# A hybrid block's kernel on one core: the decay cut by a minimum, one PE loop and all loops of the convolution written out, a normalisation moved to ACT

## The chip, the cores and the metric

The kernel runs on one core of a Trainium2 chip. The metric is device time in microseconds (us) from one launch. A core has five engines with a queue each: TensorE (PE in the profile; PEld is its weight loads), VectorE (DVE), ScalarE (ACT), GpSimd (POOL) and SyncE (SP, which only issues transfers). Each engine works through its own list in order and waits on semaphores.

## What is computed

```python
x = x + attn_a(layernorm(x))   # x: 8 x 2048 x 256
x = x + ffn(layernorm(x))
x = x + attn_b(layernorm(x))
x = x + ffn(layernorm(x))

# attn_a, the scan, per head (8 heads, P=64, N=128):
alpha = exp(dt_t * A_neg); beta = (1 - lam_t) * dt_t * alpha; gamma = lam_t * dt_t
Bx_t = u_t[:, :, :, None] * Bp_t[:, :, None, :]
h = alpha * h + beta * Bx_prev + gamma * Bx_t
y_t = einsum('bhpn,bhn->bhp', h, Cp_t)
# attn_b: projection to 3 x 256 channels, short filter of 3 taps, gates, and per channel
y = irfft(rfft(vx, n=2L) * rfft(k, n=2L))[..., :L]       # a causal convolution over 2048 tokens
# ffn:
r = sigmoid(xr @ W_r.T); k = square(relu(xk @ W_k.T)); out = r * (k @ W_v.T)
```

## The kernel before

The work is in stages that follow each other: normalise the tokens and compute the scan's parameters and the long filter (0 to 311 us); the mixer with the first feed-forward part (`mixer_and_first_ffn`); the long convolution (`long_convolution`); projection and second feed-forward part (`project_and_second_ffn`). Between stages data go through DRAM.

**Mixer.** A tile is 128 tokens, a quad is four tiles; there are 128 tiles and 32 quads. The eight heads are worked on in two groups g of four. Per tile and group POOL multiplies `steps` (L1076) out of the logarithms of the decay; PE sums them over tokens in `decay_logs` (L752, L753) and adds a mask of -30000 above the diagonal by a bf16 matmul with `ident_b` (L754); ACT takes the exponential (`exponentials`, L933) and scales the identity by rho (`own_diagonal`, L940); POOL adds the two (`add_own`, L1090); DVE multiplies the result with the Gram matrix (`weigh_gram`, L1208). Around them PE projects B and C (L744) and u (L761), DVE rotates (`rotate`, L1194, L1195), POOL adds the rotated halves (L1085), PE turns them (L769) for the Gram matrices (L779), and so on. Per quad the feed-forward part and the projection of attn_b are mixed in: `xn_over` (L826), `key` (L833), `value`, `x2n_over` (L858), `widen` (L865); DVE's `mix_tokens` (L1250) makes the `x_rk` that `key` reads. The order on each engine is written out by hand in its `body(tile, quad, n)`: `tile(q, lag, step)` calls a step for the tile that lies `lag` behind. `rounds` runs the body for four quads written out, then in a loop whose body holds two quads (14 turns), then for the last quads and two more to empty the pipeline.

**Long convolution.** 256 channels are worked on in 128 pairs. Per pair SP loads two shifted copies of the taps into one of 8 slots `toep` (`fill`), a quarter of the rows each time; DVE and ACT copy the other rows (`copy_upper`, L1369, L1370), two pairs ahead. PE transposes the signal (`signal_over`, L1482), ACT copies it (`copy_signal`, L1419), PE does 64 matmul calls over 32 lags, in the profile 128 records of each pair (`convolve`, L1498), ACT copies the odd half (`copy_odd_sums`, L1427), DVE adds the halves (`sum_halves`, L1538), PE transposes back (`back_over`, L1511), DVE adds the skip and gates (`skip_and_gate`, L1551, L1555). Four channels share a buffer `vt`, `x0t`, `yv` (four of each): in ACT's queue `store` waits until DVE has gated them, issues the store (L1412), and then `fetch` issues two loads (L1407, L1408) for the buffers that come free. All engines but POOL loop over 8 pairs per turn: the first 8 and, on all but SP, the last 8 pairs are written out.

**Last stage.** Per tile: PE projects (L1740), POOL has added a bias to the residual (L1673), DVE adds and takes the statistics (L1788 to L1795), POOL raises to the power -1/2 (L1679), DVE normalises (L1801), PE transposes (L1748), ACT copies, POOL takes differences (L1694), DVE mixes (L1809), PE multiplies (L1757, L1760, L1768), ACT and DVE finish. POOL's order is bias, difference of two tiles before, power, first column (L1687) of the tile before.

## Time and profile before

| what | value |
|---|---|
| time, median of 3 runs | 5024.38 us (5023.03 to 5030.68) |
| profiled execution | 5031.85 us, of which the span of instructions is 5030.1 us |
| mean granted TensorE clock | 0.942 of full speed |
| PE busy | 4415.2 us (88%), 40180 matmul records, and as many weight loads |
| DVE busy | 3076.4 us (61%) |
| POOL busy | 2557.7 us (51%) |
| ACT busy | 2076.3 us (41%) |

Busy time is the time in which the engine carried out instructions; semaphores, branches and the issue of transfers do not count. A name such as SPq or ACTq is the engine's queue, where transfers are issued. Behind an instruction, "idle before <-X" says how long its engine was idle just before it and what ended that; "issue" stands where nothing that the profile shows was waited for. L and a number is the line of the kernel.

### The profile page before, as it was taken

The page shows a single profiled execution, that of the slowest core. Times are in us where ns is not written, and L with a number is a line of the kernel's source. Part 1 is how long each engine was busy: PE and PEld are TensorE (multiplying, and loading weights), DVE is VectorE, ACT ScalarE, POOL GpSimd, SP SyncE. Part 2 cuts the span into 40 slices and gives each one's busy share as a digit, 9 for nine tenths or more (in the row PEclk, how much of TensorE's full clock was granted, in tenths as well). Part 3 has the DMA queues.
Part 4 walks back from the last instruction along what each step waited for, and adds up shares of the span by engine and source line. Part 5 has one row for each costly group of instructions (what it writes and reads, how often), then busy time and mean ns, then how long its engine had stood idle before and what let it go on. Part 6 is the DMA issues. An engine that isn't in the chain of part 4 may idle for free. (4 is left out here: it accounts for less than half of the span.)

```text
span 5030.1 us, 118987 instructions
## 1 busy us (share of the span) xinstructions
PE 4415.2 (88%) x40180; PEld 3573.1 (71%) x40180; DVE 3076.4 (61%) x6634; ACT 2076.3 (41%) x4921; POOL 2557.7 (51%) x3276
## 2 busy tenths in 40 slices
PE   5259999899999999999999999999668888889999
PEld 4037777777777777777777777777556777768887
DVE  8545665566656665666566665666444545459998
ACT  3123444444434444444434443444344555543333
POOL 3047666666666666676666666766200000005555
PEclk9569999999999999999999999999888999989999
DMA  8120111111111111111111111111065555543332
GB/s 265 67 78 27 40 35 43 40 41 35 44 34 39 40 35 42 39 40 35 43 40 41 35 44 34 37 40 32 28 163 138 147 148 145 142 109 97 99 100 91
DMA packets 369520, 348.52 MB, mean 69 GB/s; under 512 B 24665, under 2 KB 342937, under 8 KB 359833
## 3 DMA queue, kind: packets, MB, share of 16 engines
q1 hardware_dynamic: 250652, 273.54, 18.2%
q10 hardware_dynamic: 118272, 67.12, 5.0%
q8 instruction: 363, 5.95, 0.5%
q14 instruction: 233, 1.91, 0.1%
HBM read 231.91 MB, written 108.66 MB: 68 GB/s over the span
## 5 line engine op out<-in xcount | busy, mean ns | idle before, releaser
L744 PE MATMUL bank<-w_bc,xnT 128*128 128x512 f32 x3072 | 823.8, 410 | 85.1 <-POOL xnT L1068 40.3
L744 PEld LDWEIGHTS bank<-w_bc,xnT 128*128 128x128 f32 x3072 | 559.6, 189 | 223.0 <-issue 77.2
L949 ACT COPY turned_t<-bank 128x512 f32<-128x512 f32 x512 | 299.5, 585 | 959.8 <-PE bank L769 959.7
L1194 DVE TENSOR_TENSOR rot<-bank,par 128x512 f32<-128x512 f32 x512 | 353.2, 690 | 460.2 <-POOL turned_c L1085 245.4
L1498 PE MATMUL p_yc<-sig,toep 64*64 64x256 f32 (+14 forms) x16384 | 577.6, 293 | 57.0 <-issue 42.9
L1498 PEld LDWEIGHTS p_yc<-sig,toep 64*64 64x64 f32 x16384 | 502.0, 138 | 149.8 <-issue 106.5
L1076 POOL TENSOR_TENSOR steps<-upto,par 128x512 fp32r<-128x512 f32 x512 | 521.9, 1041 | 0.0
L1663 POOL MEMSET xT<- 128x258 f32 x1 | 0.3, 313 | 855.3 <-POOLq L1376 855.3
L1068 POOL TENSOR_TENSOR xnT<-xnT_raw,xnT 128x256 fp32r<-128x256 f32 x128 | 101.5, 793 | 542.9 <-ACT xnT L928 542.9
L1195 DVE TENSOR_TENSOR rot<-bank,par 128x512 f32<-128x512 f32 x512 | 348.5, 681 | 0.0
L1085 POOL TENSOR_TENSOR turned_b<-rot 128x512 f32<-128x512 f32 x256 | 326.1, 1274 | 41.9 <-DVE rot L1195 41.5
L1538 DVE TENSOR_TENSOR ys<-p_yc,odd_y 64x256 f32<-64x256 f32 x256 | 95.6, 411 | 402.6 <-ACT odd_y L1427 399.2
L1090 POOL TENSOR_TENSOR decay<-decay,own 128x512 f32<-128x512 f32 x256 | 329.0, 1285 | 11.3 <-ACT decay L933 10.7
L1085 POOL TENSOR_TENSOR turned_c<-rot 128x512 f32<-128x512 f32 x256 | 327.5, 1279 | 2.3 <-DVE rot L1195 2.3
L940 ACT ACTIVATE own<-ident,par 128x128 f32<-128x128 f32 x1024 | 327.4, 403 | 0.1
L865 PE MATMUL bank<-x2T,in_w 128*128 128x512 f32 x1152 | 309.7, 405 | 12.4 <-issue 5.9
L779 PEld LDWEIGHTS bank<-turned_t 128*128 128x128 f32 x2048 | 297.4, 209 | 15.8 <-issue 0.4
L1277 DVE SCALAR_TENSOR_TENSOR conv<-bank,short,conv 128x511 f32<-128x511 f32 (+1 forms) x384 | 285.9, 745 | 33.9 <-ACT conv L1005 18.8
L779 PE MATMUL bank<-turned_t 128*128 128x128 f32 x2048 | 295.9, 292 | 0.2 <-DVE u_g L1202 0.2
L1122 POOL TENSOR_TENSOR rstd<-var_eps,minus_half 128x2 f32<-128x2 f32 x128 | 90.4, 706 | 404.1 <-DVE var_eps L1234 404.1
L1208 DVE TENSOR_TENSOR mix<-bank,decay 128x512 f32<-128x512 f32 x256 | 175.5, 686 | 156.3 <-PE bank L779 156.3
L805 PEld LDWEIGHTS bank<-u_w,turned_b 128*128 128x128 f32 x2048 | 248.5, 192 | 22.1 <-issue 14.8
(258 smaller groups left out, 9780.6 us busy)
## 6 DMA issues: line engine op xcount, KB each, us to landing
toep<-taps_dram SPq DMA_DIRECT2D x256, 260.0 KB, 4.2
el<-el_dram SPq DMA_DIRECT2D x256, 128.0 KB, 3.1
xg<-arg_x SPq DMA_DIRECT2D x32, 512.0 KB, 4.7
xnT_dram<-xt_g ACTq DMA_DIRECT2D x32, 512.0 KB, 3.9
xnT_raw<-xnT_dram SPq DMA_DIRECT2D x128, 128.0 KB, 2.9
x_quad<-arg_x SPq DMA_DIRECT2D x32, 512.0 KB, 4.3
x_dram<-x_quad SPq DMA_DIRECT2D x32, 512.0 KB, 3.2
x0T_dram<-conv SPq DMA_DIRECT2D x32, 512.0 KB, 2.8
```

Of the source, the lines that this page charges most:

```text
L744: last = mm(p_bc[c][:, :], xnT[w.q % 2][p][:, k, :], w_bc[q][:, k, c * 1024 + g * W4:c * 1024 + (g + 1) * W4], start=(n == 0), stop=(n == ...
L779: last = mm(p_gram[:, c], turned_t[g][0][:, c], turned_t[g][1][:, c], start=True, stop=True)
L865: last = mm(p_post[W_BANK[e]][:, :], in_w[q][:, k, e * 128:(e + 1) * 128], x2T[p][:, k, :], start=(m == 0), stop=(m == len(SPLIT) - 1))
L940: last = s_.activation(own[g][:, h * TOK:(h + 1) * TOK], ident[:, :], ACT.Identity, scale=par[w.p][:, w.q, P_RHO + g * GROUP + h:P_RHO + g ...
L949: s_.copy(turned_t[g][c][:, :], p_tr[:, :]).then_inc(s[f"copy_{BC[c]}"], 1)
L1076: last = g_.tensor_tensor(heads(steps[p][:, :]), upto[:, :].unsqueeze(1).broadcast_to([128, GROUP, TOK]), over(of_group(P_A + p * HEADS, w ...
L1085: g_.tensor_tensor(turned(w, g, c)[:, :], rot1[c][:, :], rot2[c][:, :], ALU.add).then_inc(s[f"turn_{BC[c]}"], 1)
L1090: g_.tensor_tensor(decay[g][:, :], decay[g][:, :], own[g][:, :], ALU.add).then_inc(s["own"], 1)
L1194: v_.tensor_tensor(heads(rot1[c][:, :]), heads(p_bc[c][:, :]), cos, ALU.mult)
L1195: v_.tensor_tensor(parts(rot2[c][:, :]), parts(p_bc[c][:, :])[:, :, ::-1, :], over(sin.rearrange("p (h s) -> p h s", s=2), STATE // 2), AL ...
L1277: last = v_.scalar_tensor_tensor(out=conv[:, e, back:], in0=p_post[W_BANK[e]][:, 0:SPAN - back], scalar=short[:, e, 2 - back:3 - back], in ...
L1498: last = mm(by_seq(p_y[p][c][odd * H:(odd + 1) * H, 0:2 * TILES])[:, :, first:], toep[place % SLOTS][c * H:(c + 1) * H, lag * H:(lag + 1) ...
```

## The change

It consists of four edits.

1. The mask is no longer in the logarithms. POOL builds a constant `bound` (1 on the diagonal, 0 on one side of it, 1e38 on the other), ACT scales it by rho, held above zero by a floor of 1e-30, in place of the identity (`own_bounds`), and the exponential and this bound are joined by a minimum on DVE (`cut_decay`) in place of POOL's addition. `cut_decay` for group 1 of the tile before stands after DVE's first rotation; that for group 0 before `gate_values`. PE's mask matmul goes.
2. PE's list in the mixer is written out for all quads.
3. The convolution has no loops on any engine. SP issues the loads of `vt` and `x0t` and the stores too, between its fills.
4. In the last stage `normalise` moves from DVE to ACT, at the end of ACT's list for a tile; POOL computes `shift` = -mean * rstd for it behind the power.

```diff
-            g_.affine_select(out=t["mask"][:, :], in_=t["mask"][:, :], compare_op=ALU.is_ge, fill=0.0,
-                             base=0, pattern=[[-1, 128]], channel_multiplier=1)
             pool.drain()
-            g_.tensor_copy(t["ident_b"][:, :], t["ident"][:, :])
+            g_.tensor_tensor(t["bound"][:, :], t["upto"][:, :], t["ident"][:, :], ALU.subtract)
+            pool.drain()
+            g_.tensor_scalar(t["bound"][:, :], t["bound"][:, :], BEYOND, None, ALU.mult)
+            pool.drain()
+            g_.tensor_tensor(t["bound"][:, :], t["bound"][:, :], t["ident"][:, :], ALU.add)
...
-            v_.tensor_tensor(col(P_RHO), as3(arr["gam"][:, :]), as3(arr["e1"][:, :]), ALU.mult)
+            v_.scalar_tensor_tensor(out=col(P_RHO), in0=as3(arr["gam"][:, :]), scalar=TINY, in1=as3(arr["e1"][:, :]), op0=ALU.max, op1=ALU.mult)
...
+        if unrolled:
+            for n in range(QUADS + 2):
+                one(n, n % 2)
+            return
...
                 mm(p_arg[:, :], after_r[:, :], steps[0][:, :], start=True, stop=False)
-                mm(p_arg[:, :], after_r[:, :], steps[1][:, :], start=False, stop=False)
-                mm(p_arg[:, :], ident_b[:, :], mask[:, :].unsqueeze(1).broadcast_to([128, GROUP, TOK]),
-                   start=False, stop=True).then_inc(s["logs"], 1)
+                mm(p_arg[:, :], after_r[:, :], steps[1][:, :], start=False, stop=True).then_inc(s["logs"], 1)
...
-            rounds(pe, body)
+            rounds(pe, body, unrolled=True)
...
                 for h in range(GROUP):
-                    last = s_.activation(own[g][:, h * TOK:(h + 1) * TOK], ident[:, :], ACT.Identity,
+                    last = s_.activation(own[g][:, h * TOK:(h + 1) * TOK], bound[:, :], ACT.Identity,
                                          scale=par[w.p][:, w.q, P_RHO + g * GROUP + h:P_RHO + g * GROUP + h + 1])
...
-            def add_own(i, w, g):
-                wait_for(pool, f"diagonal{g}", i)
-                wait_for(pool, f"exp{g}", i)
-                g_.tensor_tensor(decay[g][:, :], decay[g][:, :], own[g][:, :], ALU.add).then_inc(s["own"], 1)
...
-                    tile(q, 1, add_own, 1)
...
-                    tile(q, 0, add_own, 0)
...
+            def cut_decay(i, w, g):
+
+                wait_for(dve, f"diagonal{g}", i)
+                wait_for(dve, f"exp{g}", i)
+                v_.tensor_tensor(decay[g][:, :], decay[g][:, :], own[g][:, :], ALU.min).then_inc(s["own"], 1)
...
                     tile(q, 0, rotate, 0, 1)
+                    tile(q, 1, cut_decay, 1)
                     tile(q, 0, rotate, 0, 0)
...
                     tile(q, 1, take_y, 1)
+                    tile(q, 0, cut_decay, 0)
                     tile(q, 0, gate_values)
...
+            flat = {n: t[n].rearrange("c t n -> (c t n)") for n in ("vxT_dram", "x0T_dram", "yT_dram")}
+            QUAD = U * TILES * TOK
+            rows = lambda name, m: flat[name][m * QUAD:(m + 1) * QUAD].rearrange("(u t n) -> t u n", u=U, t=TILES)
+
+            def fill(n):
+                slot = n % SLOTS
+                wait(sp, conv_ready, n - SLOTS + 1)
+                for c in range(2):
+                    src = taps[(2 * n + c) * ROW + H:(2 * n + c + 1) * ROW]
+                    sp.dma_start(toep[slot][c * H:c * H + QTR, :], bass.AP(src.tensor, src.offset, [[1, QTR], [1, SEQ + QTR]])).then_inc(toep_in[slot], 16)
+
+            def fetch(m):
+                wait(sp, yv_ready, U * (m - Q + 1))
+                sp.dma_start(vt[m % Q][:, :, :], rows("vxT_dram", m)).then_inc(quad_in[m % Q], 16)
+                sp.dma_start(x0t[m % Q][:, :, :], rows("x0T_dram", m)).then_inc(quad_in[m % Q], 16)
+
+            def store(m):
+                wait(sp, yv_ready, U * (m + 1))
+                sp.dma_start(rows("yT_dram", m), yv[m % Q][:, :, :]).then_inc(yv_out[m % Q], 16)
+
             sp.dma_start(skip[:, :], t["filt_bias"].partition_broadcast(128)).then_inc(skip_in, 16)
-
-            def fill(it, place):
-                n = BODY * it + place
-                slot, free = place % SLOTS, at(n - SLOTS + 1)
-                offs = [at((2 * n + c) * ROW + H) for c in range(2)]
-                wait(sp, conv_ready, free)
-                for c in range(2):
-                    src = taps[bass.ds(offs[c], ROW - H)]
-                    rows = bass.AP(src.tensor, src.offset, [[1, QTR], [1, SEQ + QTR]])
-                    sp.dma_start(toep[slot][c * H:c * H + QTR, :], rows).then_inc(toep_in[slot], 16)
-            for place in range(BODY):
-                fill(0, place)
-            with sp.Fori(1, ITERS) as it:
-                for place in range(BODY):
-                    fill(it, place)
+            fill(0)
+            fetch(0)
+            for n in range(1, SLOTS):
+                fill(n)
+                if n < Q:
+                    fetch(n)
+            for n in range(SLOTS, PAIRS + 2 * (Q + 1)):
+                if n < PAIRS:
+                    fill(n)
+                m = n // 2 - (Q + 1)
+                if n % 2 == 0 and m >= 0:
+                    store(m)
+                    if m + Q < QUADS:
+                        fetch(m + Q)
+            for p in range(Q):
+                sp.wait_ge(yv_out[p], 16 * QUADS // Q)
...
-            def body(it, first=False, last=False):
-                for place in range(BODY):
-                    n = BODY * it + place
-                    copy_signal(n, place % 2)
-                    if not (last and place + AHEAD >= BODY):
-                        copy_upper(act, "act", nc.scalar.copy, it, place + AHEAD)
-                    if not (first and place == 0):
-                        copy_odd_sums(n - 1, (place - 1) % 2)
-                    q = place // 2
-                    if place % 2 == 1 and not (first and q == 0):
-
-                        off, off_next, done = at((Q * it + q - 1) * QUAD), at((Q * it + q + Q - 1) * QUAD), at((Q * it + q) * U)
-                        slot = (q - 1) % Q
-                        store(off, slot, done)
-                        if not (last and q > 0):
-                            fetch(off_next, slot, done)
-            for q in range(Q):
-                fetch(q * QUAD, q, 0)
-            for place in range(AHEAD):
-                copy_upper(act, "act", nc.scalar.copy, 0, place)
-            body(0, first=True)
-            with act.Fori(1, ITERS - 1) as it:
-                body(it)
-            body(ITERS - 1, last=True)
-            copy_odd_sums(PAIRS - 1, 1)
-            store((Q * ITERS - 1) * QUAD, Q - 1, DIM)
-            for p in range(Q):
-                act.wait_ge(yv_out[p], 16 * ITERS)
+            for n in range(AHEAD):
+                copy_upper(act, "act", nc.scalar.copy, n)
+            for n in range(PAIRS):
+                copy_signal(n, n % 2)
+                if n + AHEAD < PAIRS:
+                    copy_upper(act, "act", nc.scalar.copy, n + AHEAD)
+                if n > 0:
+                    copy_odd_sums(n - 1, (n - 1) % 2)
+            copy_odd_sums(PAIRS - 1, (PAIRS - 1) % 2)
...
-            signal_over(0, 0)
-            body(0, first=True)
-            with pe.Fori(1, ITERS - 1) as it:
-                body(it)
-            body(ITERS - 1, first="last")
-            back_over(ITERS - 1, BODY - 1)
+            signal_over(0)
+            for n in range(PAIRS):
+                if n + 1 < PAIRS:
+                    signal_over(n + 1)
+                convolve(n)
+                if n > 0:
+                    back_over(n - 1)
+            back_over(PAIRS - 1)
...
-                g_.tensor_tensor(rstd[p][:, :], var_eps[p][:, :], t["minus_half"][:, 0:1], ALU.pow).then_inc(s["rstd2nd"], 1)
+                g_.tensor_tensor(rstd[p][:, :], var_eps[p][:, :], t["minus_half"][:, 0:1], ALU.pow)
+                g_.tensor_tensor(minus_mean[:, :], mean_var[p][:, 0:1], minus_one[:, :], ALU.mult)
+                pool.drain()
+                g_.tensor_tensor(shift[p][:, :], minus_mean[:, :], rstd[p][:, :], ALU.mult).then_inc(s["rstd2nd"], 1)
...
+            def normalise(g, v):
+                i, p = R * g + v, v % 2
+                wait_for(act, "rstd2nd", i)
+                wait_for(act, "xn2nd_over", i - 2)
+                s_.activation(xn[p][:, :], x3[v % R][:, :], ACT.Identity, scale=rstd[p][:, :], bias=shift[p][:, :]).then_inc(s["norm2nd"], 1)
...
+                on(0, normalise)
...
-            def normalise(g, v):
-                i, p = R * g + v, v % 2
-                wait_for(dve, "rstd2nd", i)
-                wait_for(dve, "xn2nd_over", i - 2)
-                v_.tensor_scalar(xn[p][:, :], x3[v % R][:, :], mean_var[p][:, 0:1], rstd[p][:, :], ALU.subtract, ALU.mult).then_inc(s["norm2nd"], 1)
...
-                on(0, normalise)
```

The matmul, transpose and copy steps of the convolution keep their contents; only their indices are constants now.

## Rows read from the trace of the kernel before

**Rows 1.** Busy time by stage: start:end, length, each engine's busy us (instructions), clock, DMA share, GB/s.

```profile
311.00:3652.00 3341.00, 3079.54 (x19072) 2488.24 (x19072) 1992.57 (x3651) 1403.19 (x3268) 2230.97 (x2708) 0.97 0.12 38
3652.00:4507.60 855.60, 698.91 (x17408) 592.00 (x17408) 417.91 (x1024) 432.54 (x1024) 0.27 (x2) 0.91 0.55 142
4507.60:5030.10 522.50, 508.17 (x2816) 422.36 (x2816) 464.17 (x1408) 175.95 (x512) 287.48 (x516) 0.98 0.32 97
```

The engines of these rows are PE, PEld, DVE, ACT and POOL, in this order.

**Rows 2.** Timeline of the convolution, PE's transposes: start us, length, instruction, idle before.

```profile
3690.33 0.63 PE L1482 MATMUL p_sig<-ident,vt 128*64 128x128 f32 x4
3695.32 0.63 PE L1482 MATMUL p_sig<-ident,vt 128*64 128x128 f32 x4
...
3777.81 0.70 PE L1482 MATMUL p_sig<-ident,vt 128*64 128x128 f32 x4 [3.60 <-issue]
...
4492.09 0.62 PE L1482 MATMUL p_sig<-ident,vt 128*64 128x128 f32 x4
```

**Rows 3.** Timeline, ACT's signal copy ahead of the third of these.

```profile
3775.08 0.87 ACT L1419 COPY sig<-p_sig 64x128 f32<-64x128 f32 x4 [5.57 <-issue]
```

**Rows 4.** Timeline, a stop of PE within one pair's matmuls.

```profile
3756.17 0.53 PE L1498 MATMUL p_yc<-sig,toep 64*64 64x48 f32 x22 [0.63 <-issue]
```

**Rows 5.** Timeline, PE's first convolution.

```profile
3683.36 1.13 PE L1498 MATMUL p_yc<-sig,toep 64*64 64x256 f32 x8 [12.29 <-ACT sig L1419]
```

**Rows 6.** Timeline of the mixer, PE from the logarithms to the Gram matrix.

```profile
2013.70 0.39 PE L752 MATMUL bank<-steps,after_r 128*128 128x512 f32 x1
...
2017.18 1.05 PE L779 MATMUL bank<-turned_t 128*128 128x128 f32 x8
```

**Rows 7.** Waits of PE in the mixer: us in total, times, longest.

```profile
PE bank L752 <- POOL steps L1076: 43.5, 30, 1.6
...
PE bank L833 <- DVE x_rk L1250: 29.9, 32, 3.1
```

**Rows 8.** Timeline of the last stage, one matmul group per tile.

```profile
4832.01 1.03 PE L1760 MATMUL bank<-w_r_sb,x_r 128*128 128x256 f32 x4
...
4859.94 1.03 PE L1760 MATMUL bank<-w_r_sb,x_r 128*128 128x256 f32 x4
...
4863.64 1.03 PE L1760 MATMUL bank<-w_r_sb,x_r 128*128 128x256 f32 x4
```

**Rows 9.** Timeline of the mixer, POOL's addition.

```profile
2021.82 1.26 POOL L1090 TENSOR_TENSOR decay<-decay,own 128x512 f32<-128x512 f32 x1
```

**Rows 10.** Groups by shape: busy us in all, mean ns of one, idle before.

```profile
L1801 DVE TENSOR_SCALAR xn<-x,mean_var,rstd 128x256 f32<-128x256 f32 x128 | 91.9, 718 | 1.3 <-POOL rstd L1679 1.3
...
L1290 DVE TENSOR_TENSOR vx<-conv 128x1024 f32<-128x1024 f32 x32 | 39.2, 1227 | 4.4 <-issue 3.9
```

**Rows 11.** Timeline of the mixer, first transposes of three quads in a row.

```profile
1049.50 0.63 PE L826 MATMUL bank<-ident,xn 128*128 128x128 f32 x4
...
1152.45 0.63 PE L826 MATMUL bank<-ident,xn 128*128 128x128 f32 x4
...
1254.30 0.63 PE L826 MATMUL bank<-ident,xn 128*128 128x128 f32 x4
```

**Rows 12.** Timeline: POOL in the mixer, then DVE and POOL in the last stage.

```profile
2026.32 0.70 POOL L1122 TENSOR_TENSOR rstd<-var_eps,minus_half 128x2 f32<-128x2 f32 x1
...
2027.33 0.20 POOL L1125 TENSOR_TENSOR shift<-minus_mean,rstd 128x2 f32<-128x2 f32 x1
...
4527.60 0.42 DVE L1788 TENSOR_TENSOR x<-bank,x 128x256 f32<-128x256 f32 x1 [0.43 <-PE bank L1740]
...
4529.09 0.63 POOL L1679 TENSOR_TENSOR rstd<-var_eps,minus_half 128x1 f32<-128x1 f32 x1 [0.48 <-DVE var_eps L1795]
...
4529.85 0.84 POOL L1673 TENSOR_TENSOR x<-x,out_b 128x256 f32<-128x256 f32 x1
```

**Rows 13.** Busy time in ten microseconds of the convolution, columns as in rows 1.

```profile
3700.00:3710.00 10.00, 10.00 (x273) 8.83 (x273) 4.88 (x14) 5.69 (x15) 0.00 (x0) 1.00 0.69 189
```

**Rows 14.** DMA queues: packets, MB, share of 16 engines.

```profile
q8 instruction: 363, 5.95, 0.5%
```

More of the change, by code:

```diff
@@ L491, in mixer_and_first_ffn @@
     SPAN = QUAD * TOK
-    ident, ident_b, upto, after, mask = t["ident"], t["ident_b"], t["upto"], t["after"], t["mask"]
+    ident, upto, after, bound = t["ident"], t["upto"], t["after"], t["bound"]
     w_u, w_bc = [sb(f"w_u{p}", [128, KT, 512], F32R) for p in range(2)], [sb(f"w_bc{p}", [128, KT, 2048], F32R) for p in range(2)]
@@ L640, in mixer_and_first_ffn, with rounds @@
     Place = namedtuple("Place", "n q p")
[L642 removed]
+    def rounds(eng, body, unrolled=False):
         def one(n, u):
@@ L1013, in body @@
                     tile(q, 2, square_y)
-                    tile(q, 0, own_diagonal, 0)
+                    tile(q, 0, own_bounds, 0)
                     if q == 3:
@@ L1029, in body @@
                     tile(q, 0, exponentials, 0)
-                    tile(q, 0, own_diagonal, 1)
+                    tile(q, 0, own_bounds, 1)
                     if q == 0:
@@ L1410, in store @@
-            def store(off, q, done):
-                wait(act, yv_ready, done)
-                act.dma_start(rows("yT_dram", off), yv[q][:, :, :]).then_inc(yv_out[q], 16)
             def copy_signal(n, p):
@@ L1512, in back_over @@
                 last.then_inc(back_ready, 1)
-            def body(it, first=False):
-                for place in range(BODY):
-                    nxt = (it, place + 1) if place + 1 < BODY else (it + 1, 0)
-                    prev = (it, place - 1) if place else (it - 1, BODY - 1)
-                    if not (first == "last" and place == BODY - 1):
-                        signal_over(*nxt)
-                    convolve(it, place)
-                    if not (first is True and place == 0):
-                        back_over(*prev)
-            signal_over(0, 0)
-            body(0, first=True)
-            with pe.Fori(1, ITERS - 1) as it:
-                body(it)
-            body(ITERS - 1, first="last")
-            back_over(ITERS - 1, BODY - 1)
+            signal_over(0)
[6 more added lines that the diff above has]
+            back_over(PAIRS - 1)
         @block.vector
@@ L1555, in skip_and_gate @@
                     v_.tensor_tensor(yv[q][:, 2 * p + c, :], skipped[2 * p + c][:, :], x0t[q][:, 2 * p + c, :], ALU.mult).then_inc(yv_ready, 1)
-            at_n = lambda n: n if isinstance(n, int) else dve.snap(n)
             dve.wait_ge(skip_in, 16)
-            def body(it, first=False, last=False):
-                for place in range(BODY):
-                    n = BODY * it + place
-                    if not (last and place + AHEAD >= BODY):
-                        copy_upper(dve, "dve", nc.vector.tensor_copy, it, place + AHEAD)
-                    sum_halves(n, place % 2)
-                    if not (first and place == 0):
-                        skip_and_gate(*((it, place - 1) if place else (it - 1, BODY - 1)))
-            for place in range(AHEAD):
-                copy_upper(dve, "dve", nc.vector.tensor_copy, 0, place)
-            body(0, first=True)
-            with dve.Fori(1, ITERS - 1) as it:
-                body(it)
-            body(ITERS - 1, last=True)
-            skip_and_gate(ITERS - 1, BODY - 1)
+            for n in range(AHEAD):
+                copy_upper(dve, "dve", nc.vector.tensor_copy, n)
+            for n in range(PAIRS):
+                if n + AHEAD < PAIRS:
+                    copy_upper(dve, "dve", nc.vector.tensor_copy, n + AHEAD)
+                sum_halves(n, n % 2)
+                if n > 0:
+                    skip_and_gate(n - 1)
+            skip_and_gate(PAIRS - 1)
 def project_and_second_ffn(nc, ctx, t):
@@ L1833, in build @@
         const = lambda name, dt=F32: ctx.enter_context(nc.sbuf_tensor(name, [128, 128], dt))
-        for n in ("ident", "upto", "after", "ones", "nxt", "wrap"):
+        for n in ("ident", "upto", "after", "ones", "nxt", "wrap", "bound"):
             t[n] = const(n)
-        t["mask"], t["ident_b"] = const("mask", BF16), const("ident_b", BF16)
         t["minus_half"] = ctx.enter_context(nc.sbuf_tensor("minus_half", [128, 4], F32))
```

65 lines of the change are left out of this document (25 added, 40 removed).

## The prediction

> **What bounds the kernel now.** I read the busy time by stage first [rows 1]. Three stages matter: the mixer (311 to 3652 us), the long convolution (3652 to 4508) and the last stage (4508 to 5030). In each PE is the busiest engine, but not equally: 3079.54 of 3341 us in the mixer (92%), 698.91 of 855.6 in the convolution (82%), 508.17 of 522.5 in the last. So the convolution has the most idle PE time, though two of the four edits are elsewhere.
>
> *Convolution.* I took the timeline of PE and followed one instruction that comes once per pair of channels, the transpose of line 1482 [rows 2]. Near the start, in code written out before the loop, two pairs are 3695.32 - 3690.33 = 4.99 us apart; no pair is shorter while PE works through, so 4.99 is PE's floor. From 3690.33 to 4492.09 there are 126 steps, 6.36 us on average. PE therefore loses 1.37 us per pair, 126 x 1.37 = 173 us. The long stops look like the third of rows 2: 3.60 us of idle PE. What came late is ACT's copy of the signal, which ended at 3775.95 after 5.57 us in which ACT computed nothing [rows 3]. In that time ACT's queue stood in `store` (it waits for DVE's products) and then issued three transfers. ACT is thus late because it issues, not because it is full: 432.54 us busy of 855.6 [rows 1]. A smaller kind of stop lies inside one pair's matmuls, where no semaphore is: 0.63 us before the last 22 of 128 [rows 4]. I read it as late code. The stage also starts slowly: PE's first convolution waits 12.29 us for ACT's signal copy, behind eight loads that ACT issues first [rows 5].
>
> *Mixer.* The fp32r matmuls follow each other steadily. From 2013.70 to 2017.18 there are 15 (two of the logarithms, the mask, twelve of the projection): 3.48 / 15 = 0.232 us each, the mask's among them [rows 6]. In the list of waits PE stands 43.5 us for POOL's `steps` (30 times) and 29.9 us for DVE's `x_rk` (32 times) [rows 7].
>
> *Last stage.* The matmul of line 1760 comes once per tile: 31.63 us for eight tiles, 3.954 each, but 3.70 in the one case where DVE was on time [rows 8]. DVE is busy 464.17 of 522.5 us and PE mostly waits for it.
>
> **The change part by part, in us.**
>
> 1. *Convolution: transfers to SP, no loops.* ACT no longer stands in `store` or issues; its work per pair is 432.54 / 128 = 3.4 us [rows 1], inside the 4.99. Its copies then come early in each pair. If nothing else appears, the 173 go. SP takes over: a `store` is queued behind a `fill` and waits for the gate of a pair one before the one that the fill waited for, so it holds SP briefly. Behind it stand the next fills, which have some five pairs (25 us) until they are needed; the fetches have four (20 us). Loop branches go on all engines. What I keep is the late code inside pairs. A stop of 0.63 in two pairs of five is 0.25 per pair, 127 x 0.25 = +32. Bounds: 0, and 0.63 in each pair, +80. The start gives back the 12.29 us [rows 5], -12 (0 if SP's queue fills up as ACT's did). Sum: -173 + 32 - 12 = **-153**, bounds -185 and -93.
>
>    The Trainium skill, "Runtime: NRT & Kernel Launch", section "Instruction fetch mechanics", says that fetch is sequential, that crossing a block is mostly hidden, and that a taken branch forces a fetch. By it the +32 would be nothing. The row of 0.63 in code without a branch [rows 4] does not agree with "mostly hidden", so I do not follow it.
>
> 2. *Mixer: mask matmul and POOL's add out, DVE's minimum in.* PE loses 256 matmuls (two per tile) of 0.232 us: -59. It counts almost fully, as PE is busy 92% and no other engine above 67% [rows 1]; bounds -59 and -30. POOL loses 256 adds of 1.26 us [rows 9]. At each start of a quad one of them stands ahead of the sums and of `steps`, for which PE waits 43.5 us in total [rows 7]: 30 x 1.26 = -38, bounds 0 and -43. DVE gains 256 minima of 128x512. The nearest row between two SBUF tiles is 1227 ns for 128x1024 [rows 10], 0.61 each: 157 us, DVE goes from 60% to 65%. Most lie in DVE's idle time, but before the `x_rk` for which PE waits [rows 7] one adds its full length: 32 x 0.61 = +20. `cut_decay` also waits for ACT's exponential, and behind it on DVE stand a rotation and the residual of an earlier quad. At the start of a quad ACT is late, so this delays the mix; I give it +10. Bounds for DVE together: 0, and half of the 157, +80. ACT's `own_bounds` costs what `own_diagonal` did.
>
> 3. *Mixer: PE without its loop.* The first transpose of line 826 marks a quad of tiles: 102.95 us, then 101.85 [rows 11]. They alternate so, and the loop's body holds two quads, so I read 1.10 us as the branch: 14 turns, -15; bounds 0 and -15.
>
>    Mixer: -59 - 38 + 20 + 10 - 15 = **-82**, bounds -117 and +50.
>
> 4. *Last stage: `normalise` from DVE to ACT.* DVE loses 0.718 us per tile [rows 10]: from 464.17 / 128 = 3.63 of work to 2.91. ACT is busy 175.95 of 522.5 us and holds the new operation easily. PE's floor is 3.70 [rows 8]. POOL gets a product, a drain and a second product. The same sequence in the mixer takes 2027.33 + 0.20 - 2026.32 = 1.21 us, where the power alone takes 0.70: +0.51 [rows 12]. This closes a ring: DVE's sum and statistics (4527.60 to 4529.09), POOL's power, first column and bias (4529.09 to 4530.69), then DVE's next sum. It is 3.09 now, some 0.1 more for the hand-over, so 3.19 + 0.51 = 3.70 after: level with PE. I take 3.73: 124 x (3.954 - 3.73) = **-28**, bounds -31 and -10.
>
> 5. *The constants* (POOL builds `bound` in place of the mask) and the floor under rho: three small operations more, before the first transposes need anything of them, and one operation of the same size. Nothing.
>
> Sum: -153 - 82 - 28 = -263. The profiled execution spans 5030.1 us and took 5031.85; the median of the runs is 5024.38, 7.5 lower. The span should be near 4767 and the time **4761 us**.
>
> **The rivals.**
>
> *A. As worked out*, 4761, with its own range 4700 to 4820. For it: the pairs of 4.99 exist in this trace.
>
> *B. The transfers limit the convolution.* At 5.25 us per pair the DMA engines would be busy 0.55 x 6.36 / 5.25 = 0.67 of the time, and code has to pass among them. Against it: from 3700 to 3710 they were busy 0.69 at 189 GB/s and PE worked 10.00 of 10 us [rows 13]. If two thirds of the gain stay out: 4761 + 102 = 4863.
>
> *C. The minimum takes back the mixer's gain.* DVE works in order, and a minimum that waits for ACT holds up rotations that PE needs. For it: the late ACT at each start of a quad. Against it: DVE is idle 40%. Mixer 0: 4761 + 82 = 4843.
>
> *D. The shorter stop keeps TensorE's clock up.* The granted clock is 0.97 in the mixer [rows 1]; after the stop at the start of a quad it is at the lower of its two levels for some microseconds. If it stayed at the upper one, 3% of 3341 = 100 us would come back: 4761 - 100 = 4661.
>
> *E. Slower: code written out arrives too late.* PE's mixer and convolution, and all engines of the convolution, now run through their code once. One mechanism with one price: a stop of 0.63 us [rows 4] at each piece of code. The instruction queue moved 363 packets for the larger of the two streams [rows 14]; if each cost PE another 0.73 us, the gain of 263 would be gone, and at 1 us the time is 4761 + 363 = 5124. Against it: that stream holds 5.95 MB, 74 bytes for each of PE's 2 x 40180 records, so the loops' code seems to have been moved anew on each turn already.
>
> **How the numbers follow.** A 0.60, B 0.11, C 0.13, D 0.12, E 0.04. The range 4660 to 4850 holds A, C and the upper edge of D, and leaves out most of B and D and all of E. 0.2% is about what a measurement of this kernel can tell from no change (10 us). Faster: A to D and a little of E, 0.96. Within 0.2%: 0.01. Slower: 0.03.
>
> **What the profile of the changed kernel would show.** Step 1: the transposes of the signal about 5.2 us apart, ACT without transfers, the stage some 700 us long. A spacing above 6 with stops inside the matmuls speaks for B or E, stops in front of them for a late queue of SP. Step 2: no matmul with the mask, PE's wait for `steps` far below 43.5, the quads about 100 us apart; 102 or more means C, with PE waiting for DVE's `rot` or `x_rk`; a granted clock of 0.99 or 1.00 means D. Step 3: even spacing of the quads. Step 4: 3.7 us per tile; 3.8 or more, with PE waiting behind POOL's `shift`, means that the ring closes later than I think. The prediction is wrong above all if stops inside PE's matmuls grow, or if DVE is late in the mixer.

## The result: 4827.57 us, and where the 198 us came from

The changed kernel takes 4827.57 us (median of 4 runs, 4820.36 to 4829.95), the kernel before 5025.49 in the same comparison (4 runs, 5023.03 to 5030.68): a ratio of 0.9602, with a 95% interval from 0.9586 to 0.9619. It is 198 us faster. The forecast was 4761, so 263 faster, with a range of 4660 to 4850.

The busy time by stage of the changed kernel (stretch, length, then PE, PEld, DVE, ACT and POOL busy, granted clock, DMA share, GB/s), to be read against [rows 1]:

```profile
311.00:3642.39 3331.39, 3061.74 (x18816) 2507.80 (x18816) 2150.42 (x3907) 1397.99 (x3268) 1981.20 (x2448) 0.96 0.12 38
3642.39:4329.00 686.61, 653.88 (x17408) 564.24 (x17408) 417.11 (x1024) 433.09 (x1024) 0.57 (x2) 0.98 0.66 176
4329.00:4828.20 499.20, 484.97 (x2816) 426.17 (x2816) 424.38 (x1280) 252.04 (x640) 321.58 (x773) 0.98 0.33 102
```

| stage | before | after | measured | forecast |
|---|---|---|---|---|
| mixer | 3341.0 | 3331.4 | -9.6 | -82 |
| convolution | 855.6 | 686.6 | -169.0 | -153 |
| last stage | 522.5 | 499.2 | -23.3 | -28 |

The convolution and the last stage did what was forecast. The mixer did not: PE has 256 matmuls fewer in it (18816 against 19072), POOL 260 instructions fewer, and it is hardly shorter.

*Convolution.* PE's timeline in the changed kernel, to be read against [rows 2, 5]:

```profile
3652.30 1.89 PE L1468 MATMUL p_sig<-ident,vt 128*64 128x128 f32 x8 [18.71 <-DMA x0t<-x0T_dram]
3657.07 3.36 PE L1483 MATMUL p_yc<-sig,toep 64*64 64x256 f32 x32 [2.89 <-ACT sig L1426]
...
3674.41 2.43 PE L1483 MATMUL p_yc<-sig,toep 64*64 64x184 f32 x92 [2.22 <-issue]
...
3677.17 0.62 PE L1468 MATMUL p_sig<-ident,vt 128*64 128x128 f32 x4
...
4309.54 0.63 PE L1468 MATMUL p_sig<-ident,vt 128*64 128x128 f32 x4
...
4314.54 0.63 PE L1468 MATMUL p_sig<-ident,vt 128*64 128x128 f32 x4
```

Two pairs are 4314.54 - 4309.54 = 5.00 apart when nothing stops PE, and from 3677.17 to 4314.54 there are 123 steps of 5.18 on average. The first matmul of a convolution starts 14.7 us into the stage (3657.07 - 3642.39), before 31.7 (3683.36 - 3651.68). PE's 17408 instructions of the stage take 653.88 us in place of 698.91 [rows 1], at a granted clock of 0.98 in place of 0.91: 45 of the 169 us are the same work done faster, the rest is idle time that went.

*Mixer.* PE's waits in the mixer (total, times, longest), to be read against [rows 7]:

```profile
PE bank L747 <- DVE rot L1189: 52.4, 30, 3.8
PE bank L770 <- issue: 49.8, 25, 5.1
...
PE bank L755 <- POOL steps L1077: 34.0, 31, 1.3
PE bank L834 <- DVE x_rk L1250: 27.8, 32, 3.0
PE bank L866 <- issue: 15.6, 31, 3.0
PE bank L780 <- issue: 13.5, 29, 1.3
```

The wait for `steps` fell from 43.5 to 34.0 only; the wait for `rot` is the longest of the mixer's repeated ones; and there are more waits that end on nothing shown ("issue"): 13.5 us in front of line 780, where the kernel before (its line 779) had 0.2 us of idle time in all. Not every such wait is a new one: the kernel before lost 66.8 us in front of its line 769 (the 770 here), of which the profile puts 52.5 down to ACT's `turned_t`, and run 1 below, with PE's loop, has 11.6 us in front of line 780, of which 9.9 are put down to DVE's `mix`. The quads (the four tiles between two such rows) still alternate, against [rows 11]:

```profile
1965.19 0.63 PE L827 MATMUL bank<-ident,xn 128*128 128x128 f32 x4 [0.50 <-DVE conv L1277]
...
2066.93 0.63 PE L827 MATMUL bank<-ident,xn 128*128 128x128 f32 x4 [0.50 <-issue]
2067.90 0.63 PE L827 MATMUL bank<-ident,xn 128*128 128x128 f32 x4 [0.34 <-issue]
...
2170.02 0.63 PE L827 MATMUL bank<-ident,xn 128*128 128x128 f32 x4 [0.50 <-DVE conv L1277]
```

101.74 and 103.09 us, though PE has no loop any more.

*Last stage.* PE's line 1740, once per tile, against [rows 8]:

```profile
4429.97 1.03 PE L1740 MATMUL bank<-w_r_sb,x_r 128*128 128x256 f32 x4
...
4433.70 1.03 PE L1740 MATMUL bank<-w_r_sb,x_r 128*128 128x256 f32 x4
...
4437.40 1.03 PE L1740 MATMUL bank<-w_r_sb,x_r 128*128 128x256 f32 x4
...
4441.21 1.03 PE L1740 MATMUL bank<-w_r_sb,x_r 128*128 128x256 f32 x4
...
4456.03 1.03 PE L1740 MATMUL bank<-w_r_sb,x_r 128*128 128x256 f32 x4
...
4460.00 1.03 PE L1740 MATMUL bank<-w_r_sb,x_r 128*128 128x256 f32 x4
```

Eight tiles take 30.03 us, 3.75 each: most steps are 3.70, one is 3.81 and one 3.97, once per loop turn of eight tiles. PE's weight loads waited 39.2 us in total for DVE's `x_k` before (93 times, line 1757); now they wait 12.9 (45 times, line 1737).

### The profile page after: what moved, and what is told of

The parts are those of the page before. It is cut to its first block and busy times, and to the rows that moved or that the text cites. A ratio compares the mean times of both kernels' runs of the same rounds, so it can differ in the third digit from the quotient of the medians.

```text
span 4828.2 us, 121179 instructions
## 1 busy us (share of the span) xinstructions
PE 4325.3 (90%) x39924; PEld 3566.1 (74%) x39924; DVE 3193.5 (66%) x6762; ACT 2149.7 (45%) x5049; POOL 2345.0 (49%) x3277
## 5 line engine op out<-in xcount | busy, mean ns | idle before, releaser
L1483 PE MATMUL p_yc<-sig,toep 64*64 64x256 f32 (+14 forms) x16384 | 539.6, 282 | 14.5 <-issue 10.3
L1483 PEld LDWEIGHTS p_yc<-sig,toep 64*64 64x64 f32 x16384 | 476.2, 132 | 90.9 <-issue 44.2
L1077 POOL TENSOR_TENSOR steps<-upto,par 128x512 fp32r<-128x512 f32 x512 | 537.3, 1069 | 0.0
L941 ACT ACTIVATE own<-bound,par 128x128 f32<-128x128 f32 x1024 | 326.9, 402 | 0.2 <-DMA par<-params_dram 0.2
L780 PEld LDWEIGHTS bank<-turned_t 128*128 128x128 f32 x2048 | 287.4, 206 | 52.1 <-issue 31.9
L780 PE MATMUL bank<-turned_t 128*128 128x128 f32 x2048 | 298.0, 293 | 14.3 <-issue 13.5
L866 PEld LDWEIGHTS bank<-x2T,in_w 128*128 128x128 f32 x1152 | 215.9, 192 | 74.0 <-issue 24.2
L966 ACT ACTIVATE xn<-x_quad,shift,rstd 128x256 f32<-128x256 f32 x256 | 136.7, 593 | 266.8 <-POOL shift L1121 266.8
```

Source lines behind the costliest of these rows:

```text
L780: last = mm(p_gram[:, c], turned_t[g][0][:, c], turned_t[g][1][:, c], start=True, stop=True)
L866: last = mm(p_post[W_BANK[e]][:, :], in_w[q][:, k, e * 128:(e + 1) * 128], x2T[p][:, k, :], start=(m == 0), stop=(m == len(SPLIT) - 1))
L941: last = s_.activation(own[g][:, h * TOK:(h + 1) * TOK], bound[:, :], ACT.Identity, scale=par[w.p][:, w.q, P_RHO + g * GROUP + h:P_RHO + g ...
L1077: last = g_.tensor_tensor(heads(steps[p][:, :]), upto[:, :].unsqueeze(1).broadcast_to([128, GROUP, TOK]), over(of_group(P_A + p * HEADS, w ...
L1483: last = mm(by_seq(p_y[p][c][odd * H:(odd + 1) * H, 0:2 * TILES])[:, :, first:], toep[n % SLOTS][c * H:(c + 1) * H, lag * H:(lag + 1) * H] ...
```

## The experiments

A stage ends here with SyncE's first transfer in the next; the mixer is counted from 311 us on, as above. This agrees with the table above within 1 us. All in us; the kernel before took 5024.9 to 5028.5 in the comparisons; "ratio" is to the kernel before, with its 95% interval.

| kernel | time | ratio | mixer | conv. | last |
|---|---|---|---|---|---|
| before | 5025 | 1 | 3340.7 | 855.9 | 522.5 |
| changed | 4827.6 | 0.9602 [0.9586, 0.9619] | 3331.4 | 687.6 | 498.2 |
| min_only | 4966.3 | 0.9876 [0.9860, 0.9893] | 3288.0 | 852.1 | 522.2 |
| pe_unrolled_only | 5028.9 | 1.0011 [1.0001, 1.0020] | 3378.7 | 810.7 | 522.8 |
| conv_act_issues | 4937.9 | 0.9824 [0.9808, 0.9841] | 3340.8 | 758.0 | 526.4 |
| conv_sp_issues | 4962.5 | 0.9868 [0.9852, 0.9885] | 3340.7 | 788.6 | 522.0 |
| after_pe_looped | 4779.4 | 0.9507 [0.9492, 0.9523] | 3285.5 | 682.4 | 498.0 |
| after_mixer_unrolled | 4799.3 | 0.9541 [0.9525, 0.9557] | 3300.1 | 688.9 | 499.0 |
| min_mask_kept | 5023.7 | 0.9990 [0.9981, 1.0000] | 3335.1 | 852.5 | 522.2 |
| no_mask_only | 4962.8 | 0.9874 [0.9857, 0.9890] | 3284.0 | 833.1 | 522.0 |
| no_add_only | 5390.5 | 1.0729 [1.0707, 1.0750] | 3694.6 | 856.8 | 529.5 |
| no_add_free | 4996.4 | 0.9947 [0.9930, 0.9963] | 3295.5 | 854.9 | 529.2 |
| conv_code_moved | 5056.8 | 1.0064 [1.0043, 1.0085] | 3340.1 | 883.9 | 522.1 |
| last_stage_unrolled | 4776.7 | 0.9512 [0.9491, 0.9532] | 3285.1 | 684.9 | 491.9 |

**1. min_only.** Of the change only the mixer's arithmetic: mask out, minimum on DVE; all loops stay.

```diff
-                mm(p_arg[:, :], after_r[:, :], steps[1][:, :], start=False, stop=False)
-                mm(p_arg[:, :], ident_b[:, :], mask[:, :]..., start=False, stop=True).then_inc(s["logs"], 1)
+                mm(p_arg[:, :], after_r[:, :], steps[1][:, :], start=False, stop=True).then_inc(s["logs"], 1)
...
-                    tile(q, 1, add_own, 1)      # POOL
...
+                    tile(q, 1, cut_decay, 1)    # DVE
...
```

> The kernel before with one part alone: the mask matmul and POOL's add are gone from the mixer and DVE takes the minimum; all loops stay, the convolution and the last stage are as before. Theory T (in each second quad of tiles DVE's and ACT's loop branches of about 3 and 2 us stand on PE's path, and what PE saves elsewhere is waited off there, partly as a longer stretch at the lower clock): the mixer is 8 to 12 us shorter than before, all of it in the quads written out. Rival P (the terms of my prediction): 67 us shorter. Rival C (the minimum on DVE takes the gain back): 0 or longer, with PE waiting more for rot and x_rk in every quad, written out or not.

The mixer became 52.7 us shorter. Theory T falls, rival C too; the prediction's term (67) was nearly right in size. So what the changed kernel lacks is lost by the other part.

**2. pe_unrolled_only.** Of the change only PE's mixer without its loop.

```diff
-            rounds(pe, body)
+            rounds(pe, body, unrolled=True)
```

> The kernel before with one part alone: PE's mixer without its loop; mask matmul, POOL's add, the convolution and the last stage as before. Theory T: the mixer is 0 to 2 us shorter and the quads still alternate by 1.1 us, because it is DVE's and ACT's branch that makes them alternate. Rival P: 15 us shorter and the quads evenly spaced.

Neither: the mixer is 38.0 us longer. Quads in the stretch where the other engines loop are 103.0 and 105.2 us apart, before 101.8 and 102.9. PE's 19072 instructions take 3107.54 us in place of 3079.54 [rows 1]: 28 of the 38 are the same work done slower, 10 are idle. The granted clock of the turn quad shows it. First this kernel, then the kernel before (stretch, length, PE busy, granted clock, DMA share, GB/s):

```profile
2138.00:2143.00 5.00, 1.61 (x10) 1.00 0.04 11
2143.00:2154.00 11.00, 8.24 (x42) 0.53 0.20 61
2154.00:2160.00 6.00, 6.00 (x42) 1.00 0.00 0
```

```profile
2123.00:2129.00 6.00, 2.68 (x12) 1.00 0.01 3
2129.00:2133.00 4.00, 3.07 (x11) 0.57 0.53 164
2133.00:2140.00 7.00, 7.00 (x58) 1.00 0.00 0
```

After its stops at the start of the quad PE works for 11 us almost wholly at the lower of its two levels (1.2 GHz), where the looped PE had 4. Over the whole mixer the clock is 0.95 against 0.97 [rows 1]. The stop in front is longer, 3.39 us for DVE's `rot` against 2.47, and DVE itself stands there for its own loop's turn ("issue"), as it did before. Again this kernel first:

```profile
2140.41 0.69 DVE L1198 TENSOR_TENSOR rot<-bank,par 128x512 f32<-128x512 f32 x1 [3.19 <-issue]
...
2141.85 1.67 PE L748 MATMUL bank<-w_bc,xnT 128*128 128x512 f32 x6 [3.39 <-DVE rot L1199]
```

```profile
2122.32 0.69 DVE L1194 TENSOR_TENSOR rot<-bank,par 128x512 f32<-128x512 f32 x1 [3.04 <-issue]
...
2123.66 1.67 PE L744 MATMUL bank<-w_bc,xnT 128*128 128x512 f32 x6 [2.47 <-DVE rot L1195]
```

The convolution, whose code is the same, is 45 us shorter at the same time, which hides the loss in the total; run 11 follows that up.

**3. conv_act_issues.** Of the change only the convolution without loops, on all engines; ACT issues as before. With the loops go three semaphore increments of PE per pair (`pe_go`), here as in the change; they cost nothing that shows, since pairs that have them are 4.99 us apart where nothing stops PE [rows 2] and pairs without them 5.00. Against the changed code:

```diff
             for n in range(PAIRS):
                 copy_signal(n, n % 2)
...
+                m = n // 2 - 1
+                if n % 2 == 1 and m >= 0:
+                    store(m)
+                    if m + Q < QUADS:
+                        fetch(m + Q)
```

> The kernel before with the convolution alone changed: no loops on any engine, but ACT still waits for the gate's products and issues the stores and fetches at the places where it did. Theory S (ACT's store and issue are the stop, the loops are small): the stage goes from 856 to between 800 and 845 us. Rival L (the loops and their registers cost the time): the stage comes to 700 or less.

**4. conv_sp_issues.** SyncE issues everything, written out; PE, ACT and DVE keep their loops of eight pairs.

```diff
             for q in range(Q):
-                fetch(q * QUAD, q, 0)          # ACT
...
-                        store(off, slot, done)
-                        if not (last and q > 0):
-                            fetch(off_next, slot, done)
...
```

> The kernel before with the convolution alone changed: SyncE issues all transfers, written out; PE, ACT and DVE keep their loops of eight pairs. Theory S: the stage goes from 856 to between 695 and 740 us, the loop turns costing at most 14 x 3 us over the 687 of the changed kernel. Rival L: 780 or more.

Run 3 came to 758.0 us and run 4 to 788.6: theory S is wrong in both, rival L in the first. Without the loops the stage loses 97.9 us, with ACT freed 67.3; together 165.2, and the change brought 168.3. The two causes add up. How the sum splits is less sure than these figures look, since run 11 shows that a looped convolution can differ by tens of microseconds though its own code is the same. Of the 97.9, 33.8 us are PE's work at a higher clock (665.14 us busy at 0.96 in place of 698.91 at 0.91), the rest is idle time. PE's waits in the stage, of the kernel before, of conv_act_issues and of conv_sp_issues:

```profile
PE p_sig L1482 <- issue: 47.9, 12, 5.0
PE p_yc L1498 <- issue: 42.9, 48, 2.6
```

```profile
PE p_yc L1476 <- ACT sig L1409: 45.1, 40, 11.6
...
PE p_yc L1476 <- issue: 16.7, 18, 3.1
```

```profile
PE p_sig L1490 <- issue: 52.8, 13, 4.7
...
PE p_yc L1506 <- issue: 14.1, 27, 3.0
```

With the loops there are 12 or 13 stops of about 4 us at the first instruction of a turn. The stop of 3.60 us that the prediction took as its example [rows 2] is one of them: it is the transpose for pair 17, the first instruction of PE's second turn, and by the kernel it needs ACT's copies up to pair 15, not the copy for pair 16 that came late [rows 3]. With ACT freed, such stops stay (52.8 us); without the loops 2.2 us are left of them. Without the loops, but with ACT issuing, PE waits 40 times for ACT's signal copy.

**5. after_pe_looped.** The changed kernel, only PE's mixer looped again (run 2's line the other way round).

> The changed kernel with one part undone: PE's mixer has its loop again. Theory M (it is the mixture, PE written out while DVE and ACT still turn in loops, that costs the mixer 43 us): the mixer spans 3288 us as in the run with the minimum alone, the convolution and the last stage stay at 687 and 499, and the time is 4785. Rival N (the convolution profits from the written-out mixer, as it did by 45 us in the run with PE alone): the convolution grows to 700 or more and the time stays above 4800.

It came as theory M had it: 3285.5, and 4779.4 us in total, 48 less than the changed kernel. Whether the mixture is the reason is for run 6. Rival N does not hold: the convolution stays at 682.4.

**6. after_mixer_unrolled.** The changed kernel with `unrolled=True` for all five engines of the mixer.

> The changed kernel with the mixer written out on all five engines. Theory M (loop turns of DVE and ACT are the cost, and none are left): quads 100 to 101 us apart throughout, the mixer 3275 to 3295, the time 4770 to 4790. Rival F (written-out code reaches PE too late, wherever it is used): quads of 102 or more, the mixer at 3331 or above, small stops of PE that wait for nothing shown, the time 4828 or above.

Between the two: 3300.1, with quads from 100.3 to 101.9. So of the 45.9 us that PE's written-out list costs, 31.3 go when the other engines are written out too (theory M's mixture), and 14.6 stay. PE's waits over the same 2000 us (1100 to 3100) of the changed kernel, of after_pe_looped and of after_mixer_unrolled:

```profile
PE bank L747 <- DVE rot L1189: 37.5, 19, 3.8
PE bank L770 <- issue: 24.8, 14, 2.4
...
PE bank L780 <- issue: 8.8, 19, 0.7
PE bank L866 <- issue: 7.2, 20, 0.4
PE bank L827 <- issue: 7.1, 24, 0.5
```

```profile
PE bank L747 <- issue: 37.7, 20, 3.1
PE bank L770 <- ACT turned_t L950: 24.6, 10, 2.5
...
PE bank L780 <- DVE mix L1208: 7.7, 19, 0.7
PE bank L747 <- DVE rot L1189: 4.5, 10, 0.5
```

```profile
PE bank L770 <- issue: 46.1, 19, 2.4
...
PE bank L747 <- DVE rot L1189: 7.6, 19, 0.4
```

PE's own turn (37.7) costs nothing of its own: without it PE waits 37.5 at the same line, one group of matmuls later, for DVE, which is in its turn. With it the two turns fall together: at one turn the looped PE stands 0.94 and 2.84 us at its own branch and then finds `rot` there, where PE without a loop stands 3.49 us for it. Written out on all engines that wait is 7.6, but 21.5 us of it come back one step later, in front of line 770 (46.1 in place of 24.6). What the written-out PE adds are the small stops at lines 780, 866 and 827: 23.1 us, of which the looped PE has only the 7.7 at line 780. What they wait for no view shows; that it is late code is a guess. In the timeline above line 827's eight transposes begin with a stop and are split by another; in the looped kernel they follow each other without one.

**7. min_mask_kept.** The kernel before with POOL's add replaced by DVE's minimum; the mask matmul stays. (Mask and minimum together leave out the diagonal's weights.)

```diff
-                    tile(q, 1, add_own, 1)      # POOL
...
+                    tile(q, 1, cut_decay, 1)    # DVE
...
```

> The kernel before with POOL's add replaced by DVE's minimum, the mask matmul kept; all loops, the convolution and the last stage as before. Theory Q (PE's own work decides: 256 matmuls of 0.232 us are the gain of the run with the minimum alone): the mixer within 10 us of before, 3331 to 3345. Rival R (POOL's add in front of the sums and the steps was the gain): the mixer 25 to 45 us shorter.

**8. no_mask_only.** The kernel before without the mask matmul.

```diff
-                mm(p_arg[:, :], ident_b[:, :], mask[:, :]..., start=False, stop=True).then_inc(s["logs"], 1)
```

> The kernel before without the mask matmul and nothing else: the weights above the diagonal are not cut, so part of the computation is left out. Theory Q: the mixer 45 to 60 us shorter than before. Rival R: 0 to 25 us shorter, PE then waiting that much longer for POOL's steps and ACT's copies.

3335.1 and 3284.0, that is -5.6 and -56.7: both as theory Q has them. But run 7 alone can't tell "both small" from "both large and opposite", hence the next two.

**9. no_add_only.** POOL's add out, nothing in its place.

```diff
-                    tile(q, 1, add_own, 1)
...
-                wait_for(dve, f"own{g}", i)
+                wait_for(dve, f"diagonal{g}", i)
+                wait_for(dve, f"exp{g}", i)
-                wait_for(act, f"own{g}", i - 1)
+                wait_for(act, f"mix{g}", i - 1)
```

> The kernel before without POOL's add of own and nothing in its place (DVE's weighing waits for the exponential instead): the weights of the diagonal are left out. The mask matmul stays. Prediction's term (each of 30 quads starts 1.26 us earlier): the mixer 25 to 43 us shorter. Theory Q (PE's own work decides, POOL's add was hidden): within 10 us of before. If the add was worth something and DVE's minimum costs as much, the mixer here is shorter than the 3335.1 us of the run with mask and minimum by that price.

It tells nothing about the add, since the edit brought a wait of its own: the mixer is 353.9 us longer. From 1100 to 3100 us ACT shows

```profile
ACT own L940 <- DVE mix L1202: 387.6, 141, 5.0
```

Here ACT's `own_diagonal` waits until DVE has weighed the tile before, and the copies that PE needs stand behind it.

**10. no_add_free.** The same, without that last wait.

```diff
-                wait_for(act, f"mix{g}", i - 1)
```

> The run without POOL's add once more, but ACT's own_diagonal no longer waits for DVE's weighing (nothing reads its result any more); in the run before, that wait alone held ACT for 388 us of 2000. The weights of the diagonal are left out. Prediction's term for the add: the mixer 25 to 43 us shorter than before. Theory Q (the add was hidden): within 10 us of before. Against the 3335.1 us with mask and minimum, this run gives the price of DVE's minimum: 0 to 10 us by theory Q, 30 by the prediction.

The mixer is 45.2 us shorter than before. Theory Q falls in its second half: the add was on the path, as the prediction said (38), and DVE's minimum costs 3335.1 - 3295.5 = 39.6 us (the prediction: 20 + 10). In run 7 they cancel. Each of the two figures holds, besides the operation, ACT's wait for it before it writes `own` again, which this run dropped too.

PE's waits show where the two act. Of this run, for `steps` and `x_rk` over the mixer:

```profile
PE bank L752 <- POOL steps L1075: 31.8, 30, 1.4
PE bank L833 <- DVE x_rk L1243: 30.2, 32, 3.3
```

Without the add the wait for `steps` is 11.7 us shorter [rows 7] and that for POOL's `y_sum` 13.4 (2.9 in place of 16.3): these are the places that the prediction named, with 25 us in place of 38. Another 17.7 us are PE's work, done faster (3061.84 in place of 3079.54). With the minimum (run 7) the wait for `x_rk` stays at 30.1, so the 20 us that the prediction put there did not come. What came is 12.3 us more of waiting for `steps` (44.1), 12.0 more for DVE's `conv` at lines 835 and 874, and 16.3 us more of PE's work (3078.17). POOL's `steps` themselves take 1124 ns each in run 7 against 1041 in this one and before, though POOL's code for them is the same.

The time fell by less (28.5 by the medians), partly because the last stage, though not changed, took 529.2 in place of 522.5: its step at the loop turn is 4.5 us in place of 3.9, once per eight tiles; why is open.

**11. conv_code_moved.** The kernel before with 24 transposes of PE ahead of the convolution.

```diff
+            for _ in range(24):
+                tp(p_sig[0][0:H, 0:TOK], ident[:, 0:H], ident[:, :])
             signal_over(0, 0)
```

> The kernel before with 24 more transposes of PE ahead of the convolution's first one, where PE waits 26 us for its first data anyway: they cost no time there and only move the code behind them. Theory K (the looped convolution takes longer or shorter by where its code lies, which is why the same code took 810.7 to 855.9 us in five kernels): the stage changes by more than 10 us, in the waits for nothing shown. Rival (it depends on how the engines stand to each other at the stage's start): 845 to 860.

The stage takes 883.9 us, 28.0 more, and the time 31 more. The transposes themselves cost nothing: the first matmul of a convolution starts 31.8 us into the stage, before 31.7. PE's waits in it, against those of the kernel before under run 4:

```profile
PE p_yc L1498 <- issue: 70.5, 60, 4.8
PE p_sig L1482 <- issue: 55.6, 13, 5.1
PE p_yc L1498 <- DVE toep L1370: 22.4, 8, 3.7
```

The stops that wait for nothing shown grew from 90.8 to 126.1 us, as theory K had it, and the rival's 845 to 860 did not come. That the cause is the place of the code is argued from what the 24 transposes change; no run moved the code in another way.

**12. last_stage_unrolled.** after_pe_looped with the last stage written out on all engines.

```diff
-        with eng.Fori(1, TILES // R) as g:
-            for u in range(R):
-                body(lambda lag, step: step(g, u - lag))
+        for g in range(1, TILES // R):
+            for u in range(R):
+                body(some(g, u))
```

> The changed kernel with PE's mixer looped again and the last stage written out on all engines. Theory M (the loop turn costs the last stage 0.4 us every eight tiles: 3.97 and 3.80 in place of 3.70): last stage 490 to 495, the time 4772 to 4776. Rival F (written-out code comes late): the last stage at 498 or above and stops of PE in it that wait for nothing shown.

The last stage takes 491.9, 6.1 less, with nearly every tile at 3.70; theory M holds. The time, 4776.7, can't be told from run 5's 4779.4. The two are the fastest kernels here.

```profile
4387.54 1.03 PE L1740 MATMUL bank<-w_r_sb,x_r 128*128 128x256 f32 x4
...
4417.17 1.03 PE L1740 MATMUL bank<-w_r_sb,x_r 128*128 128x256 f32 x4
```

## Why the prediction was right, and where it was wrong

**Step 1, convolution: -169.0, forecast -153. Right in sum, wrong in attribution.** The floor of 4.99 per pair (it is 5.00) and what stays above it (5.18 in place of my 5.25) carried the number. The stops of 0.63 were rarer than I took them to be (13 at the pairs' matmuls, 10.3 us in all, in place of 32), and the start gave 17 us in place of 12. From 3690.33 (pair 2) to 4492.09 (pair 127) there are 125 steps and not 126, so 6.41 each and 178 us lost, not 173. But I put the 173 us down to ACT's issuing, and "loop branches go on all engines" got no price. Runs 3 and 4 give one: 98 us for the loops, 67 for ACT. That the change took away both is why the sum held, and that is luck: with ACT's part alone (run 4) the stage is at 788.6. The stop that I read as ACT's lateness was PE's loop turn. And I took the time per pair from spacings alone, which hid that 45 us of the gain would be a higher clock.

**Step 2, mask and minimum: the run with it alone gives -52.7, forecast -59 - 38 + 20 + 10 = -67.** Each term was near in size: the mask matmuls -56.7, the add -45.2, the minimum +39.6. Measured one by one they sum to -62.3, together they give 10 less. The mask's mechanism is right: PE's busy time falls by 57.8 us without it (3021.79 in run 8). The add's is right for 25 us of it (run 10). The minimum's is not: the wait for `x_rk`, where I put +20, did not grow, and its cost came in other places, so that this term's size is luck.

**Step 3, PE without its loop: +38.0 alone and 3331.4 - 3285.5 = +45.9 beside the minimum, forecast -15. This step failed.** I read the alternation of 102.95 and 101.85 [rows 11] as PE's branch, because PE's loop body holds two quads. So does DVE's, and it is DVE that stands 3 us at each turn; PE waits there in any case. Nor does the alternation measure a branch: in run 8 all loops stay, and its quads are 100.9 and 100.5 apart. Two things came instead, in proportions that differ: beside the old arithmetic mostly a longer stretch at the lower clock (28 of 38 us), beside the new one mostly idle time (28.7 of 45.9; PE busy is 3061.74 with and 3044.53 without the written-out code). Nearly the whole miss of 65 us is this step, 15 + 46 = 61; the misses of the others nearly cancel (step 1 gave 16 more than forecast, step 2 gave 14 less, step 4 gave 5 less).

By the Trainium skill, "Runtime: NRT & Kernel Launch", section "Instruction fetch mechanics", a taken branch whose target is not at hand forces a fetch, and this is given as a reason to write code out. The convolution agrees in that PE stood about 4 us at each turn and does not without the loops (98 us for all of it); whether it stood for a fetch no trace shows. The mixer does not bear out the advice: PE's branch there is hidden behind DVE's, and PE's written-out code stops where nothing is shown to be waited for (line 827, 0.34 us in the middle of its transposes). So I was right not to take crossings for free in step 1, and wrong to forget them in step 3.

**Step 4, last stage: -23.3, forecast -28.** 3.75 per tile in place of 3.73; what is above 3.70 is the loop turn, as run 12 shows. The ring of DVE and POOL does not close above 3.70.

**The rivals.** B did not come: 0.66 of DMA and 176 GB/s at 5.18 us per pair. C's time (4843) is nearest to the result of all, and the signs that I had named for it came (quads above 102, PE waiting longer for `rot`), but its mechanism is not the cause: with the minimum and a looped PE (run 1) 30 quads take 3457.01 - 432.24 us, 100.8 each. The minimum does take back a gain, 39.6 us, but that of the add and not that of the mask. The sign was badly chosen, since DVE's turn gives the same picture. D did not come: the granted clock of the mixer is 0.96. Of E, written-out code did cost time, in one stage and far below E's price: 45.9 us in the mixer, of which 14.6 are left when no engine loops. That this is code coming late is argued, not shown.

## What to carry to other kernels

An engine's loop turn costs what it adds behind the turns of the others: before unrolling one engine, look for which engine PE stands at the turn, and price the unrolled engine alone. Where several engines turn together and PE waits for them anyway, leave PE's loop; where all can be written out it may bring more than the transfers that one wanted to move, as in the convolution, or lose 14.6 us, as in the mixer (3300.1 against 3285.5 with all loops kept), so measure it per stage. And two parts of a change that nearly cancel look like two parts that do nothing; run each alone, and look at what wait the experiment itself brings in.

## What the runs showed of the hardware that was not expected

The looped convolution, the same code in the same order, took from 810.7 to 883.9 us in eight kernels that differ only in what stands ahead of it, and 24 transposes in PE's idle time made it 28.0 us longer. Written out, it took 682.4 to 688.9 in four. A gain of 40 us in a looped stage next to an edit in another may be this.

A stop of PE of 3.39 us in place of 2.47 went with 11 us at the lower clock in place of 4, and 7 us more at half speed are 3.5 us of work. That the longer stop is the cause is what the rows suggest; no run changed the stop alone.

POOL's multiplication of `steps` took 1124 ns in place of 1041, 512 times, once DVE had a minimum of two tiles to take (run 7 against run 10). That the two engines hinder each other is argued; no run set them apart in time.
